# GpSimd's product of H and half the degrees, written as one of two tensors instead of one with a scalar per partition

## The reference

```python
def gnn(X, edge_index, W_root, W_neigh, b):      # X is the layer-normed x
    row, col = edge_index
    deg = segment_sum(ones, row)
    denom = maximum(deg, 1.0)[:, None]
    neigh_mean = segment_sum(X[col], row) / denom
    H = relu(X @ W_root + neigh_mean @ W_neigh + b)
    diffs = abs(H[row] - H[col]) ** 2.0
    return tanh(segment_sum(diffs, row) / denom)
```

## Time and profile before, and how to read it

| | |
|---|---|
| Time, median of 3 runs | 2998.78 us (2998.61 to 3006.76) |
| Time of the profiled execution | 2996.17 us |
| Its span in the profile | 2993.9 us |
| Granted TensorE clock, mean | 0.838 |
| Busy: PE, DVE, ACT, POOL | 82%, 68%, 30%, 70% of the span |
| Stage H | about 1360 us to 1427 us of the span |

### The profile page before, as it was taken

How to read it: one execution, slowest core, us unless ns; L and a number is a source line. 1 busy time by engine, 2 the same in 40 slices (tenths; PEclk the granted TensorE clock), 3 DMA queues, 4 the chain that set the end, 5 groups by cost and what they waited for, 6 DMA issues and landing times.

```text
span 2993.9 us, 33585 instructions
## 1 busy us (share of the span) xinstructions
PE 2449.1 (82%) x9139; PEld 1398.2 (47%) x9139; DVE 2023.9 (68%) x5339; ACT 892.2 (30%) x2489; POOL 2098.2 (70%) x2132
## 2 busy tenths in 40 slices
PE   6664678778778787879798889899888897888995
PEld 3553344444444444447233333333333333787995
DVE  8998655555555555555677777777777778476654
ACT  4698000000000000004233333333333333555553
POOL 5487777777777777778777777777777773325666
PEclk7555777777777777779899999999999999999997
DMA  1524333333333333332533333333333334344555
GB/s 36 172 38 95 106 105 105 105 105 106 106 105 105 105 105 106 106 106 89 179 104 111 105 104 105 105 104 105 104 104 105 104 104 142 99 125 133 149 152 151
DMA packets 172859, 329.41 MB, mean 110 GB/s; under 512 B 42449, under 2 KB 108605, under 8 KB 172675
## 3 DMA queue, kind: packets, MB, share of 16 engines
q0 software_dynamic: 100416, 249.69, 29.6%
q1 hardware_dynamic: 68610, 73.93, 7.5%
q10 hardware_dynamic: 3648, 3.67, 0.4%
HBM read 275.37 MB, written 42.53 MB: 106 GB/s over the span
## 4 chain that ended last, share of the span: by engine, by line
PE 40%; DVE 17%; POOL 12%; DMA 12%; issue 11%; DVEq 4%; ACT 3%; POOLq 0%; SPq 0%; ACTq 0%
PE ps L1212 22%; POOL arena L1179 11%; DVE big L1251 9%; PE ps L2067 7%; DMA arena<-xn_table,graph 6%; DMA arena<-h_table,graph 5%; DVEq L1222 4%; PE ps L2041 3%; DVE graph L1245 2%; PE ps L1342 2%; ACT big L697 1%; PE ps L645 1%; PE ps L1271 1%; PE ps L2019 1%; ACT arena L1192 1%
## 5 line engine op out<-in xcount | busy, mean ns | idle before, releaser
L1212 PE MATMUL ps<-arena,graph 128*128 128x258 f32 (+3 forms) x3956 | 1692.3, 597 | 340.6 <-DVE graph L1245 329.4
L1212 PEld LDWEIGHTS ps<-arena,graph 128*128 128x128 f32 (+1 forms) x3956 | 766.7, 225 | 1254.4 <-DVE graph L1245 1006.6
L1251 DVE TENSOR_TENSOR big<-ps,big 128x258 f32 (+1 forms) x1978 | 1099.0, 556 | 136.0 <-PE ps L1212 101.5
L1179 POOL DMA_INDIRECT arena<-h_table,graph x842 | 805.6, 957 | 259.1 <-issue 135.1
L1179 POOL DMA_INDIRECT arena<-xn_table,graph x842 | 796.7, 946 | 266.2 <-issue 194.4
L1245 DVE TENSOR_SCALAR graph<-iota,graph 128x128 f32<-128x128 f32 x1684 | 502.4, 298 | 593.3 <-DMA arena<-xn_table,graph 374.7
L1192 ACT ACTIVATE arena<-arena 128x256 f32<-128x256 f32 x842 | 348.3, 416 | 714.7 <-DMA arena<-h_table,graph 714.4
L1280 ACT ACTIVATE late<-ps 128x256 f32<-128x256 f32 x49 | 18.8, 383 | 950.4 <-PE ps L1261 950.4
L1639 POOL DMA_INDIRECT arena<-xn_table,node x118 | 123.2, 1044 | 188.8 <-PE ps L2019 136.3
L587 POOL DMA_INDIRECT edge_list<-big x64 | 142.6, 2228 | 42.9 <-issue 42.3
L645 PE MATMUL ps<-big,arena 128*128 128x128 f16 x832 | 98.9, 308 | 57.6 <-ACT big L697 39.1
(11 more groups left out here) (320 smaller groups left out, 1786.5 us busy)
## 6 DMA issues: line engine op xcount, KB each, us to landing
y_table<-big SPq DMA_DIRECT2D x57, 256.0 KB
arena<-xn_table,graph POOLq DMA_INDIRECT x842, 2.8
arena<-h_table,graph POOLq DMA_INDIRECT x842, 2.8
big<-graph SPq DMA_DIRECT2D x1, 8480.0 KB, 28.9
h_table<-node SPq DMA_DIRECT2D x7, 896.0 KB, 4.0
node<-in_x SPq DMA_DIRECT2D x1, 6144.0 KB
late<-h_table SPq DMA_DIRECT2D x12, 512.0 KB, 4.9
xn_table<-big SPq DMA_DIRECT2D x12, 512.0 KB, 4.4
```

What stands on the lines that cost most here:

```text
L1179: e.indirect_dma_start(out=row, out_offset=None, in_=table, in_offset=bass.IndirectOffsetOnAxis(ap=idx[:, t:t + 1], axis=0)).then_inc(s_ro ...
L1212: e.matmul(out_, hot[part, g % HOTS, :], moving, start=True, stop=True).then_inc(s_sum[i], 1)
L1251: e.tensor_tensor(block, ps[a % BANKS][:, 0:width], block, ALU.add)._wait_ge(s_sum[i], a + 1).then_inc(s_add[i], 1)
```

## The change

POOL's product of H and `deg` is written as `tensor_tensor` with the degrees broadcast along the 256 features (a step of zero in that dimension) instead of `tensor_scalar` with one scalar per partition. Same engine, same place in the order, same semaphore, same numbers. The 49 memsets stay, and the masks of the edge sort on POOL (L576) stay `tensor_scalar`.

```diff
             for b in range(NB):
                 e.memset(by_block[:, b, D:W2], 0.0)
                 e.wait_ge(s_h, b + 1)
-                e.tensor_scalar(by_block[:, b, 0:D], node[:, b, :], deg[:, b:b + 1], None, ALU.mult).then_inc(s_mclr, 1)
+                e.tensor_tensor(by_block[:, b, 0:D], node[:, b, :], deg[:, b:b + 1].to_broadcast([P, D]),
+                                ALU.mult).then_inc(s_mclr, 1)
```

## The result

The changed kernel takes **2992.73 us** in the median of 20 runs (2991.10 to 2999.26). The kernel before, in 20 runs timed with it, takes 3001.77 (2996.00 to 3009.31). The ratio of the two is 0.9976, with a 95% interval of 0.9969 to 0.9982: 0.24% faster, or 7 us; the medians alone are 9.0 us apart. The profiled execution has a span of 2990.2 us (before: 2993.9).

What follows compares the result with a forecast made beforehand. The two edge passes fill most of the span; stage H ends on PE's pace and the last store, not POOL. Gain on the path 0, so 2996.2 us profiled stays and the median is forecast at 2998.8 us, range 2993 to 3006.

Steps and rivals of the forecast that it cites:

- The chain of stage H: PE's products at 1.18 us a block, DVE's addition, ACT's last relu, H's last store, then POOL's first gather of pass 1.
- the slack: Stage H: POOL could end 2.78 us later over 49 blocks, 0.057 a block, at no cost.
- a shorter product frees nothing there: Stage H: no shortening moves pass 1's first gather forward, since the store is still last; gain on the path 0.
- x: Length of one two-tensor product on POOL in stage H, taken as 0.75 us.
- the 9 forecast: Stage H: POOL waits some 0.19 us for ACT in each of 49 blocks, 9 us of new idle time.
- The bound from below: POOL's product takes at least 0.55 us, from L1624's shortest on the same shape with two operations and two scalars.
- The change touches none of that: The two edge passes and POOL's issue of gathers, most of the 2993.9 us span, were taken as unaffected.
- 1 (x over 1.01): Stage H: two-tensor product exceeds the slack, POOL becomes the bound; +20 us, 3019 us; chance 0.04.
- 3: Stage H: a shorter product relieves SBUF traffic slowing DVE, ACT or stores; about 2988 us; chance 0.01.
- 2: Stage H: POOL's second input holds a port against DVE, deciding from 0.41 us a block; 3015 us; chance 0.03.
- a POOL that waits for the relu would meet DVE less: Stage H, argument against the port hold: L1303 ends before the relu which releases POOL, 1401.28 against 1401.47.

Runs made afterwards that it cites:

- two_op: Kernel before, its scalar product on POOL given a second operation that adds 0.0; ratio 1.0012 (1.0000 to 1.0023).
- last_tt: Kernel before with 48 scalar products kept and only the 49th made a two-tensor product; 3401.33 us, ratio 1.0005 (0.9989 to 1.0020).

## Why the prediction was wrong

*What held.* The chain of stage H, the slack, and the claim that a shorter product frees nothing there: 67.0 us before, 67.6 after, the gather released by the last store. x was 0.613, between the bounds of 0.55 and 1.84, and 0.14 under the 0.75 taken. POOL's new idle time is 20.6 us, against the 9 forecast plus the 4.7 already there. The bound from below held as a bound only for that form: two_op shows 0.478 for the scalar product with a second operation, so the row's 0.550 was not even its shortest.

*The step that failed* is in the first paragraph: "The change touches none of that". "That" was the two passes and their gathers. I took the gathers of pass 1 as given because their code, their queue and their order don't change. They changed by 11 ns each, 842 times, on the engine whose instructions are the pace of that pass. The sum had no term for it; measured, it is -8.7 us of pass 1 in the profile.

*Could it have been seen?* In part. The groups on the page of the profile have the row: 957 ns for the gathers of pass 1, and beside it, in the same list, 946 for those of pass 0. It is the same line, the same shape and the same number of instructions. Nothing in that trace says that the products of stage H are the cause. But an unexplained 11 ns, times 842, on the pace-setting engine, with the edited instructions standing between the two groups, would have deserved a rival of its own on the faster side, 9 us, which is just what was missing: the range's low end of 2993 left it out.

*The rivals.* 1 (x over 1.01) is out. 3 had the sign and named about 2988 us, but for another reason, in stage H, which did not get shorter. 2 happened in small: DVE's L1303 is held in part of the blocks. The group of L1303 in the stage with a product of POOL around one L1303 of the kernel before (the L1303 at 1400.93 in the earlier trace rows), then the group and the timeline of the changed one:

```profile
L1303 DVE TENSOR_SCALAR arena<-big,rden 128x256 f32<-128x256 f32 x49 | 17.0, 351 | 0.0
...
1400.67 0.92 POOL L1322 TENSOR_SCALAR big<-node,deg 128x256 f32<-128x256 f32 x1
```

```profile
L1303 DVE TENSOR_SCALAR arena<-big,rden 128x256 f32<-128x256 f32 x49 | 21.0, 432 | 0.0
...
1401.78 0.31 POOL L1320 MEMSET big<- 128x256 f32 x1
...
1401.91 0.34 DVE L1303 TENSOR_SCALAR arena<-big,rden 128x256 f32<-128x256 f32 x1
1402.65 0.42 DVE L1315 TENSOR_TENSOR arena<-ps,node 128x256 f32<-128x256 f32 x1 [0.40 <-PE ps L1343]
1402.99 0.53 DVE L1303 TENSOR_SCALAR arena<-big,rden 128x256 f32<-128x256 f32 x1
```

Every other one now takes 0.53 us instead of 0.34: it starts inside POOL's product (1402.52 to 1403.13) and runs over its end into the memset. The others lie beside a memset alone and take 0.34. I had argued that a POOL that waits for the relu would meet DVE less. It does overlap it less: in the kernel before, an L1303 of 0.35 us lies wholly inside a product and is not held. What counts is the place of the overlap: inside a product L1303 takes 342 to 358 ns in the kernel before (44 of 49), and over the end of one 533 or 534 in the changed kernel (22 of 49). The hold of 0.19 us stays under the 0.41 from which the rival decides, and L1315 and the pace of PE are as before.

*The threshold.* I set 0.3% as what a measurement of this kernel can tell from no change, from three runs. With 20 runs of either kernel the interval is 0.13% wide in all, and a shift of 0.24% is clear. A base of three runs also sat 3 us under the median of 20 (2998.78 against 3001.77).

## What to carry to other kernels

Where one engine's short instruction, repeated many hundred times, sets the pace of a stage, its duration is a term of every sum, also of a change elsewhere on that engine: compare its median between stages, and treat a difference of 1% that nothing explains as a cost that an edit may move. To learn what moves it, look also at instructions that ran before the edited ones: where they changed too, a state left behind is not the whole cause. A forecast that "nothing on the path changes" is then worth a rival on either side, of the size of count times that difference. And a gain of a few nanoseconds an instruction should be timed in more than one job: with gathers of 946 or 947 ns in all four, the change gained 0.24% in two jobs (in one with a small memset added) and lost 0.2 to 0.3% in two others.

## What the runs showed of the hardware

- POOL's indirect gather of 128 rows has a median of 946 to 949, 954, or 957 to 960 ns over 842 in a row, depending on the kernel and the pass. Within a pass the median of every 105 gathers stays within 2 ns. With no extra product ahead of pass 0, pass 1 is 10 to 11 ns longer than pass 0 where the last product of stage H is a one-operation scalar product, and within 1 ns of it where it is not. The scatters ahead of all these products differ between kernels too, by 6 ns (1540 against 1546), so it is not shown that the products leave a state behind.
- The one-operation scalar product on POOL is the slow form: 922 ns at its shortest for 128x256 in f32, against 613 for two tensors and 478 (mean) with a second operation that adds 0.0.
- A memset of one element per partition between two gathers costs 1 ns of pass time: 0.12 us of work fit in the 0.30 us pause.
- DVE's 128x256 scalar product (L1303) is not held while it lies inside POOL's one-operation product: 342 to 358 ns in the kernel before. Where it runs over the end of a product of POOL into the memset behind it, it takes 533 or 534 ns in the changed kernel and 632 to 811 in last_tt.
- In jobs where this kernel takes 3350 to 3400 us instead of 3000, the passes stop about every 25 us, and there the sign of this change turned (ratios 1.0030 and 1.0017).
